# Edge stage of a four-layer graph network: the second product and the denominators divided anew among VectorE, GpSimd and TensorE

## What is computed

```python
H = x @ weight.T
alpha_src = jnp.sum(H * att_src[0], axis=-1)
alpha_dst = jnp.sum(H * att_dst[0], axis=-1)
C = alpha_src[None, :] + alpha_dst[:, None]
Tau = adj_matrix.T * jnp.exp(jnp.maximum(0.2 * C, C))
att_weights = Tau / jnp.sum(Tau, axis=1, keepdims=True)
Z = adj_matrix.T * att_weights @ H
...
x = _layernorm(x + _L3_gnn_ref(x, adj, L3_gnn_weight, L3_gnn_att_src, L3_gnn_att_dst), axis=-1)
```

## Time and profile before

| what | value |
|---|---|
| runs | 11073.33, 11077.53, 11080.54 us; median 11077.53 |
| profiled execution, span | 11077.6 us (first to last instruction; the page gives no other time for it) |
| TensorE's mean granted clock | 0.982 of 2.4 GHz |
| edge stage, first tau to the last product's end | 10839.4 to 11040.8 us |
| busy shares of the whole span | PE 90%, DVE 89%, ACT 93%, POOL 72% |
| busy in 10839.4 to 11034.9 (195.5 us) | PE 184.7, DVE 194.6, ACT 153.1, POOL 0.0 us |

### The profile page before, as it was taken

One profiled execution on the slowest core, in us unless ns is written; L12 is line 12 of the kernel. 1 busy time (PEld: TensorE's weight loads), 2 busy tenths in 40 slices (PEclk: granted clock), 3 DMA queues, 4 the chain that ended last, 5 costly groups with the idle time before them and its releaser, 6 DMA issues. The chain is left out here.

```text
span 11077.6 us, 307002 instructions
## 1 busy us (share of the span) xinstructions
PE 9989.2 (90%) x115286; PEld 4513.5 (41%) x115286; DVE 9834.5 (89%) x9022; ACT 10277.8 (93%) x7161; POOL 7988.9 (72%) x3346
## 2 busy tenths in 40 slices
PE   5859999999999999899999999998999999999988
PEld 5525543333333333333333333333333333333383
DVE  7469989999999999899999999998999999999958
ACT  3559999999999999999999999999999999999916
POOL 0038878888888888788888888887888888888800
PEclk8979999999999999999999999999999999999999
DMA  9997743333333332433333333335332333333264
GB/s 389 319 226 101 100 84 50 50 49 48 48 50 50 50 49 48 94 50 49 48 48 50 50 50 49 48 48 95 50 49 48 49 50 50 49 49 47 46 209 176
DMA packets 426842, 902.84 MB, mean 82 GB/s; under 512 B 86887, under 2 KB 349038, under 8 KB 379790
## 3 DMA queue, kind: packets, MB, share of 16 engines
q1 hardware_dynamic: 426732, 901.33, 40.5%
HBM read 745.35 MB, written 155.64 MB: 81 GB/s over the span
## 5 line engine op out<-in xcount | busy, mean ns | idle before, releaser
L1209 DVE SCALAR_TENSOR_TENSOR a_probs<-ps,adj_ring 128x1024 f32<-128x1024 f32 x7488 | 8855.1, 1220 | 777.3 <-PE ps L1097 633.4
L1183 POOL TENSOR_TENSOR a_pool_probs<-a_pool_probs,adj_ring 128x1024 f32<-128x1024 f32 x3328 | 7972.6, 2396 | 1884.3 <-ACT a_pool_probs L1167 1877.7
L1170 ACT ACTIVATE a_probs<-a_probs 128x2048 f32<-128x2048 f32 (+1 forms) x3328 | 8701.1, 2615 | 42.9 <-DVE a_probs L1209 42.7
L1167 ACT ACTIVATE a_pool_probs<-ps 128x1024 f32<-128x1024 f32 x3328 | 5012.0, 1506 | 49.1 <-PE ps L1097 49.1
L1097 PE MATMUL ps<-a_q,a_k 34*128 34x512 f32 (+1 forms) x21632 | 4091.5, 445 | 806.5 <-ACT a_pool_probs L1167 614.6
L1117 PE MATMUL ps<-a_probs,a_v 128*9 128x256 f32 x59904 | 3860.2, 380 | 0.0
L1097 PEld LDWEIGHTS ps<-a_q,a_k 34*128 34x128 f32 x21632 | 1794.5, 185 | 3477.0 <-ACT a_pool_probs L1167 1631.1
L1117 PEld LDWEIGHTS ps<-a_probs,a_v 128*9 128x9 f32 x59904 | 1579.3, 91 | 1602.0 <-issue 201.4
L1117 PE MATMUL ps<-a_pool_probs,a_v 128*9 128x256 f32 x26624 | 2068.1, 382 | 1.5 <-POOL a_pool_probs L1183 1.5
L1117 PEld LDWEIGHTS ps<-a_pool_probs,a_v 128*9 128x9 f32 x26624 | 395.4, 88 | 974.2 <-issue 937.6
L602 POOL MEMSET v_rows<- 128x512 f32 x2 | 1.9, 1038 | 403.6 <-POOLq L90 403.6
(11 more groups left out here) (174 smaller groups left out, 2177.6 us busy)
## 6 DMA issues: line engine op xcount, KB each, us to landing
a_k<-k_parts SPq DMA_DIRECT2D x1664, 208.0 KB
a_q<-q_parts SPq DMA_DIRECT2D x3072, 16.0 KB
a_v<-v_ext SPq DMA_DIRECT2D x384, 117.0 KB, 2.1
adj_t<-tr SPq DMA_DIRECT2D x26, 1664.0 KB, 20.7
g0tile<-adj_t SPq DMA_DIRECT2D x26, 1664.0 KB, 9.6
g2tile<-adj_t SPq DMA_DIRECT2D x26, 1664.0 KB
nat<-in_adj SPq DMA_DIRECT2D x25, 1663.5 KB, 18.8
e_nat<-in_adj SPq DMA_DIRECT2D x25, 1663.5 KB, 7.0
```

What stands on the lines that cost most here:

```text
L1167: nc.scalar.activation(probs(k), score(j), ACT.Exp, scale=SCALE).then_inc(scores_exped, 1)
L1170: nc.scalar.activation(sums_of(k), sums_of(k), ACT.Exp, scale=2.0).then_inc(sums_exped, 1)
L1183: nc.gpsimd.tensor_tensor(beside(c, probs(k)), beside(c, probs(k)), adj_of(c, j), ALU.mult).then_inc(multiplied, 1)
L1209: v.scalar_tensor_tensor(out=beside(c, probs(k)), in0=beside(c, score(j)), scalar=SCALE / 2, in1=adj_of(c, j), op0=ALU.mult, op1=ALU.add). ...
```

## The change

Two constants and the division of work in `edge_phase`. `DEN_COLS` goes from 768 to 384: TensorE sums 4 x 384 = 1536 columns of tau, in matmuls of 256 and 128 columns. The other 1792 are added to `e_den_of`, which grows to that width, and by GpSimd now, in the place of VectorE. `BOTH_COLS` = 2560 divides the second product: VectorE makes columns 0 to 2559, GpSimd the last 768. A new semaphore `rest_ready` tells of GpSimd's part. TensorE waits for it ahead of the last two matmuls of a block, SP ahead of a load, and VectorE waits for GpSimd's add (`rest_added`) of the block two back before it writes tau again. Behind the last block TensorE has 3 transposes of column sums in the place of 6, and 14 matmuls of `e_den_of` in the place of 2.

```diff
--- before.py
+++ after.py
@@ -45,7 +45,8 @@
 TILE_BUFS = 3
 ACC_BUFS = 3
 O_BUFS = 6
-DEN_COLS = 6 * P
+DEN_COLS = 3 * P
+BOTH_COLS = 5 * BANK
 LEAK = 0.2
 
 CHUNKS = ((24, 2), (0, 8), (8, 8), (16, 8))
@@ -1547,6 +1548,7 @@
         padded, chain, src_ready = mem.sem("e_padded"), mem.sem("e_chain"), mem.sem("e_src_ready")
         cut, exped, tau_ready, both_ready, rest_added = (mem.sem("e_" + s) for s in (
             "cut", "exped", "tau_ready", "both_ready", "rest_added"))
+        rest_ready = mem.sem("e_rest_ready")
         summed, weighed = mem.sem("e_summed"), mem.sem("e_weighed")
         z_copied, z_turned, den_copied, den_turned, den_read, joined = (mem.sem("e_" + s) for s in (
             "z_copied", "z_turned", "den_copied", "den_turned", "den_read", "joined"))
@@ -1560,6 +1562,7 @@
         def _(sp):
             for i in range(EDGE_LOADS, BLOCKS):
                 sp.wait_ge(both_ready, i - EDGE_LOADS + 1)
+                sp.wait_ge(rest_ready, i - EDGE_LOADS + 1)
                 edge.load(sp, adj, i)
             mid = BLOCKS // 2
             sp.wait_ge(norm.normed, 1)
@@ -1587,6 +1590,8 @@
                 pe.wait_ge(both_ready, i + 1)
                 for at in range(0, NP, BANK):
                     to = min(at + BANK, NP)
+                    if at == BOTH_COLS:
+                        pe.wait_ge(rest_ready, i + 1)
                     ins = nc.tensor.matmul(ps[:, at:to], h[0:rows, i, :], both[i % 2][0:rows, at:to],
                                            start=begin and to < NP, stop=end, skip_group_check=True)
                 ins.then_inc(weighed, 1)
@@ -1627,6 +1632,18 @@
                 nc.gpsimd.memset(nat[b][:, N:NP], 1.0).then_inc(padded, 1)
             nc.gpsimd.memset(den_of[:, :], 0.0).then_inc(padded, 1)
             nc.gpsimd.memset(ones[:, :], 1.0).then_inc(padded, 1)
+            pool.wait_ge(padded, EDGE_LOADS + 2)
+            for i in range(BLOCKS):
+                b, rows = i % 2, rows_of[i]
+                pool.wait_ge(tau_ready, i + 1)
+                if i >= 2:
+                    pool.wait_ge(weighed, i - 1)
+                nc.gpsimd.tensor_tensor(both[b][0:rows, BOTH_COLS:NP], tau[b][0:rows, BOTH_COLS:NP],
+                                        nat[i % EDGE_LOADS][0:rows, BOTH_COLS:NP], ALU.mult).then_inc(rest_ready, 1)
+                if i >= 1:
+                    pool.wait_ge(rest_added, i)
+                nc.gpsimd.tensor_tensor(den_of[0:rows, :], den_of[0:rows, :], tau[b][0:rows, 4 * DEN_COLS:NP], ALU.add
+                                        ).then_inc(rest_added, 1)
 
         @block.vector
         def _(dve):
@@ -1643,21 +1660,19 @@
                 dve.wait_ge(edge.loaded[i % EDGE_LOADS], loads[i % EDGE_LOADS])
                 if i >= 2:
                     dve.wait_ge(summed, i - 1)
+                    dve.wait_ge(rest_added, i - 1)
                 v.tensor_tensor(tau[b][0:rows, :], edges[b][0:rows, :], nat_i[0:rows, :], ALU.mult).then_inc(tau_ready, 1)
                 dve.wait_ge(tau_ready, i + 1)
                 if i >= 2:
                     dve.wait_ge(weighed, i - 1)
-                v.tensor_tensor(both[b][0:rows, :], tau[b][0:rows, :], nat_i[0:rows, :], ALU.mult).then_inc(both_ready, 1)
-                if i >= 1:
-                    dve.wait_ge(rest_added, i)
-                v.tensor_tensor(den_of[0:rows, :], den_of[0:rows, :], tau[b][0:rows, 4 * DEN_COLS:NP], ALU.add
-                                ).then_inc(rest_added, 1)
+                v.tensor_tensor(both[b][0:rows, 0:BOTH_COLS], tau[b][0:rows, 0:BOTH_COLS], nat_i[0:rows, 0:BOTH_COLS],
+                                ALU.mult).then_inc(both_ready, 1)
             dve.wait_ge(summed, BLOCKS)
             dve.wait_ge(weighed, BLOCKS)
-            v.tensor_copy(den_rows[:, :], ps[:, NP:8 * BANK]).then_inc(den_copied, 1)
+            v.tensor_copy(den_rows[:, :], ps[:, NP:NP + DEN_COLS]).then_inc(den_copied, 1)
             v.tensor_copy(z_t[:, half:NP], ps[:, half:NP]).then_inc(z_copied, 1)
             dve.wait_ge(den_turned, 1)
-            turned = ps[:, NP:8 * BANK].rearrange("p (k c) -> p c k", c=P)[:, 0:P:32, :]
+            turned = ps[:, NP:NP + DEN_COLS].rearrange("p (k c) -> p c k", c=P)[:, 0:P:32, :]
             v.reciprocal(den[:, 0:4 * DEN_COLS // P].rearrange("p (g k) -> p g k", g=4), turned).then_inc(den_read, 1)
             v.reciprocal(den[:, 4 * DEN_COLS // P:BLOCKS], ps[:, NP + 1:NP + 1 + rest // P]).then_inc(den_read, 1)
             dve.wait_ge(den_read, 2)
```

## The result

| | before | changed |
|---|---|---|
| runs, median | 11075.43 us (4 runs) | 11187.15 us (4 runs, 11181.15 to 11191.91) |
| ratio | | 1.0099, 95% interval 1.0088 to 1.0111 |
| profiled execution, span | 11077.6 us | 11186.1 us |
| tau to tau in the steady state | 7.53 us | 11.69 us |
| first tau to the end of the span | 238.2 us | 346.8 us |

The change makes the kernel slower by 1%, 112 us by the medians and 108.5 by the two profiled spans. The whole difference lies in the edge stage: its first tau starts at 10839.3, as before at 10839.4.

A forecast was written before the change was run, and what follows sets the result against it. VectorE was taken to bound the edge stage at 7.53 us a block; with turns 12.5, so 124.3 us up to the last tau plus 3.9 for last block and tail, 128.2 together: 11206 us, 8 in 10 between 11120 and 11240.

The forecast's parts named there:

- What bounds the kernel: Edge stage: VectorE sets the period of 7.53 us a block; TensorE would hold at about 7.28.
- the unknown price: Edge stage: cost of GpSimd working beside VectorE, from nothing up to the sum, 6.44 + 5.99 = 12.43 us a block.
- turns: Edge stage: VectorE and GpSimd never overlap, each block costs their sum; 12.5 us a block, 11206 us total, chance 0.67.
- the row of the attention stage: VectorE's L1209 takes 1220 ns beside busy GpSimd, as L617 does with GpSimd idle; it speaks for free overlap.
- B: Rival, edge stage: no contention, TensorE's period of 6.61 us, 11057.5 us, or 11051.4 if VectorE's 6.40 decides; chance 0.17.
- C: Rival, edge stage: SBUF path shared by the word, not the instruction; 10.4 us a block, +76 us, 11154; chance 0.16.
- the sign named beforehand: Edge stage trace: with turns one of tau, both and GpSimd's two groups is stretched or a gap precedes it; under C all four.
- D: On top of the forecast: TensorE, busy 53%, gets a lower clock; up to 11232 us, within the range, no separate chance.
- The steady block: Edge stage, tau to tau: 12.43 us of VectorE's and GpSimd's work plus hand-overs give 12.5 us, against 7.53 before.
- the hand-overs: Edge stage: four changes between dependent instructions a block, 0.02 to 0.03 us each; at 0.15 they would add 13 us.
- The last block: End of edge stage: last tau to the end of TensorE's product grows from 13.2 to 13.8 us, +0.6.
- The tail: After the last product: den_of's matmuls +3.6 us, last add +0.4, copy -0.4, transposes -0.3; with the last block +3.9.

The follow-up runs named there:

- PSUM experiment: Changed kernel with the second operand of VectorE's tau and both in PSUM (ones), adj left out, TensorE's 128-column sums group left out: 11055.66 us.
- memset experiment: Changed kernel with GpSimd's two products replaced by memsets of the same regions, so GpSimd only writes SBUF: 11063.14 us.
- add-alone kernel: Changed kernel with VectorE making all 3328 columns of both and GpSimd only adding the 1792 columns: 11175.33 us.

## Why the prediction was right, and where it was off

**What bounds the kernel, and the choice at the unknown price:** right. The forecast chose turns over the row of the attention stage, where overlap is free, because that row has one SBUF operand on VectorE. The PSUM experiment shows that this difference decides, and the memset experiment that GpSimd's reading is the other half. One of the reasons given did not hold: that GpSimd has a single way into SBUF was read from two operands costing it 2.34 ns a column where writing costs 0.83, but one operand costs it no less (4.72 us for 1792 columns against 3.96 with two), so that pace says nothing of the ways. The rule of the Trainium skill, SBUF — State Buffer, section Who interferes with whom, gave the same end of the range, and the traces agree with it in each part that was tried: two SBUF inputs (5.3 us a block, none with one), reading and not writing, the whole instruction for GpSimd's two-operand instructions (7.41 us of tau behind an add). Beside each of its one-operand instructions 1.3 us of VectorE's work ran all the same; there the traces and the rule differ, and the measurement decides.

**Rivals.** B did not come true; its period did, 6.57 measured with memsets for 6.61 worked out. C, 10.4 us a block, fell with the add-alone kernel. The changed kernel alone would not have told the two apart by the sign named beforehand: all four groups are stretched (5.22 for 3.62 us, 6.51 for 2.82, 4.39 for 1.83, 7.39 for 3.96), which the prediction had put down to C. Each waits for the rest of its neighbour's turn; what tells turns from sharing is the ends, and both at 3.62 us in the add-alone kernel. D was there and small: the granted clock went to 0.82, and the second product, 5.85 us at full clock, took up to 8.90 (5.85 in four of the 26). Except in the last block, nobody waits for it.

**The steady block**, 12.5 us predicted, 11.69 measured, is the term that was mis-sized. From the ends read above, the four turns are 3.49 us for tau, 3.86 for the add, 2.68 for both and 1.66 for GpSimd's part of both: 11.69. The sum had 3.62, 4.19, 2.82, 1.80 and 0.07 for the hand-overs. VectorE's two are 0.27 shorter: an instruction that has waited needs less from its release on than by itself. GpSimd's two are 0.47 shorter. Of this, 0.13 is the length of a 1024-column instruction spread over the columns, 5.99 us, where the two take 1.83 + 4.03 = 5.86 in the PSUM kernel; the other 0.34 is about twice GpSimd's fixed part of 0.18 us (worked out at the end), which lies outside the turn. The hand-overs cost nothing that can be seen. The sum allowed 2 us in total for a fixed part; all this took 25 x 0.8 = 20.

**The first block**, taken like the others, cost nothing: tau to tau 6.40 us, as GpSimd had no earlier work in hand.

```profile
10839.34 3.62 DVE L1664 TENSOR_TENSOR e_tau<-e_edge,e_nat 128x3328 f32<-128x3328 f32 x1 [7.58 <-ACT e_edge L1622]
10843.00 2.82 DVE L1668 TENSOR_TENSOR e_both<-e_tau,e_nat 128x2560 f32<-128x2560 f32 x1
10845.74 5.24 DVE L1664 TENSOR_TENSOR e_tau<-e_edge,e_nat 128x3328 f32<-128x3328 f32 x1
```

That is 5.3 us less. With it the last tau starts 98.8 us later than before, not 124.3.

**The last block**, +0.6 predicted, came to +6.1 (11138.17 + 7.54 - 11126.4 = 19.3 against 13.2). The sum let GpSimd's part of both be the last and only two banks of the product stand behind it. In fact tau waited 1.6 us for GpSimd, both was served behind the add and ended at 11138.1, and the whole product stood behind both, 7.54 us where it was 5.85. The window of this last product has a granted clock of 0.77 of the full 2.4 GHz, behind 2.17 us without a matmul; before, the stage had 0.98.

```profile
11138.20:11145.70 7.50, 7.50 (x14) 3.14 (x14) 0.00 (x0) 0.00 (x0) 5.50 (x2) 0.77 0.00 0
```


**The tail**, +3.3 predicted without the last block, measured +3.6: the 28 records of den_of took 4.68 us from their first weight load to that of the next group, 0.17 each, 4.15 more than the 4 before; the copy is 0.56 us and not 0.96; the transposes 3 and not 6. The wait of 0.4 us for the last add did not come, it ends at 11143.7, before the product. 98.8 + 6.1 + 3.6 = 108.5, the difference of the spans.

So the total is nearer to the forecast than its parts: up to the last tau it is 25.5 us short, behind it 5.8 us long (9.7 for 3.9). That these two have opposite signs is luck.

## What to carry to other kernels

Before work is moved to GpSimd, count SBUF operands: beside a VectorE instruction with one of its two operands in SBUF it was free, and writing alone was free even beside two; reading beside two, a column of GpSimd's two-operand work cost VectorE 2.11 ns, twice what VectorE needs for it, so for such float32 work no division between the two pays while VectorE is the bound, and work taken from an engine that had time for it is a pure loss. A busy share near 100% on both engines with stretched durations is how such turns look: compare each line's median with its minimum or with the same form where the neighbour idles.

No version here that does all the work beats the kernel before. The two that took less, 11055.66 and 11063.14 against 11070.95 us, leave out the adjacency in VectorE's products, or GpSimd's products and sums; and PSUM, which the kernel fills with Z and the sums, has no place for a VectorE operand of 3328 columns. And the prize is small: with TensorE's sums left as they were, its 7.28 us a block by the earlier trace rows lie 0.25 under VectorE's 7.53, 6 us in all; with them halved, the prediction's rival B put it at 20 to 26 us.

## What was not expected of the hardware

- With GpSimd's two-operand instructions, the turn is handed over at each instruction's end to the engine that waits, also where the other has its next instruction ready (the add between two pieces of tau: 4.75 us, in place of 7.39).
- What GpSimd takes of VectorE's time is in proportion to its columns, 2.11 ns each at 256, 768 and 1792, without the fixed part of 0.18 us that its lengths without contention show (1.83 us for 768 columns and 4.03 for 1792, so 2.15 ns a column).
- GpSimd's instructions with one operand are no quicker by themselves (4.72 us for 1792 columns, 3.96 with two) and hold up VectorE too, but 1.3 us of VectorE's work run beside each, at 768 and at 1792 columns: 3.7 us a block in the place of 5.3.
